# A four-layer graph network on one core: slot weights read from a PSUM bank, the last block's edges all on its list, the last-but-one update moved into the last turn

## The reference

```
s = x @ msg_w[:, :D].T ;  d = x @ msg_w[:, D:].T
messages = gelu(s[:, None, :] + d[None, :, :] + msg_b)
aggregated = einsum('ijd,ij->id', messages, adj)          # only where adj is not 0
new = concatenate([x, aggregated]) @ upd_w.T + upd_b
h = gelu(new) + x
out = layernorm(layernorm(h) * ln_w + ln_b + x)           # the layer's, then the network's
```

## Time and profile before

| | us |
|---|---|
| median of 3 runs | 740.55 (735.58 to 743.03) |
| the profiled execution's own time | 736.55 |
| its span, first to last instruction | 734.8 |
| layer 3's gathers, first to last | 445.91 to 709.27 |
| the last layer norm's end (DVE) | 728.0 |

### The profile page before, as it was taken

How to read it: one execution, slowest core, us unless ns; L and a number is a source line. 1 busy time by engine, 2 the same in 40 slices (tenths; PEclk the granted TensorE clock), 3 DMA queues, 4 the chain that set the end, 5 groups by cost and what they waited for, 6 DMA issues and landing times.

```text
span 734.8 us, 6845 instructions
## 1 busy us (share of the span) xinstructions
PE 455.6 (62%) x1987; PEld 268.9 (37%) x1987; DVE 503.4 (69%) x1592; ACT 302.4 (41%) x362; POOL 378.1 (51%) x499
## 2 busy tenths in 40 slices
PE   4122015999959999999998368665345542675211
PEld 3121012444425565544446356443133321433100
DVE  3409904998971754997054586899898879877744
ACT  3566256356942523399836031123223223322213
POOL 7303630667561030667000665777777777777740
PEclk9555555799989999999999759877567766655555
DMA  8999993799980020499601232212221222212200
GB/s 330 336 427 424 401 413 77 270 406 401 392 336 10 1 76 1 151 383 424 275 1 43 66 91 63 51 48 59 56 55 50 56 58 58 56 48 58 55 15 14
DMA packets 33211, 120.06 MB, mean 163 GB/s; under 512 B 8704, under 2 KB 19892, under 8 KB 24148
## 3 DMA queue, kind: packets, MB, share of 16 engines
q1 hardware_dynamic: 20258, 80.99, 28.0%
q0 software_dynamic: 10176, 38.57, 16.7%
q10 hardware_dynamic: 2734, 0.01, 0.2%
HBM read 114.00 MB, written 5.55 MB: 163 GB/s over the span
## 4 chain that ended last, share of the span: by engine, by line
PE 39%; POOL 20%; DMA 15%; DVE 10%; issue 8%; ACT 3%; SPq 3%; ACTq 0%; POOLq 0%
PE ps L121 37%; POOL G L919 16%; DMA ring<-in_adjT_dram 13%; POOL Go L919 4%; SPq L839 2%; DVE agg L1824 1%; DMA xT_s<-in_xT_dram 1%; PE ps L1254 1%; PE ps L1260 1%; ACT binT L998 1%; DVE G L1821 1%; PE ps L1375 1%; DVE I L1500 1%; DVE listed L1708 1%; DVE V L1510 0%
## 5 line engine op out<-in xcount | busy, mean ns | idle before, releaser
L919 POOL DMA_INDIRECT G<-near,IX x154 | 159.5, 1036 | 46.9 <-issue 46.3
L121 PE MATMUL ps<-ring,hwu 128*128 128x512 f32 (+3 forms) x264 | 114.7, 588 | 1.0 <-ACT hwu L1011 1.0
L121 PE MATMUL ps<-ring,xT_s 128*128 128x512 f32 (+2 forms) x264 | 106.9, 547 | 1.8 <-DMA ring<-in_adjT_dram 1.8
L121 PE MATMUL ps<-ident,agg 128*128 128x128 f32 (+1 forms) x44 | 14.9, 435 | 123.4 <-DVE agg L1824 123.4
L1500 DVE FIND_INDEX8 I<-V,rows 128x8 uint32<-128x340 f32 (+2 forms) x176 | 88.2, 504 | 0.0
L1510 DVE MAX8 V<-rows 128x8 f32<-128x340 f32 (+2 forms) x176 | 85.6, 497 | 0.8
L121 PE MATMUL ps<-E,M 128*128 128x321 f32 (+2 forms) x192 | 66.1, 505 | 16.8 <-DVE IO L1716 9.9
L121 PEld LDWEIGHTS ps<-ring,hwu 128*128 128x128 f32 (+1 forms) x264 | 51.3, 204 | 64.4 <-issue 63.3
L998 ACT ACTIVATE binT<-ring 128x2708 bf16<-128x2708 f32 (+1 forms) x22 | 53.9, 2457 | 47.5 <-DMA ring<-in_adjT_dram 47.5
L942 POOL DMA_DIRECT2D rows<-in_adj_dram x18 | 10.8, 603 | 120.5 <-DVE I L1500 120.5
L121 PE MATMUL ps<-u,binT 128*128 128x4 bf16 (+1 forms) x484 | 18.2, 167 | 82.7 <-ACT binT L998 82.7
(11 more groups left out here) (255 smaller groups left out, 858.5 us busy)
## 6 DMA issues: line engine op xcount, KB each, us to landing
ring<-in_adjT_dram SPq DMA_DIRECT2D x48, 1354.0 KB, 16.8
rows<-in_adj_dram POOLq DMA_DIRECT2D x17, 1354.0 KB, 10.3
rows<-in_adj_dram SPq DMA_DIRECT2D x4, 1354.0 KB, 23.3
G<-near,IX POOLq DMA_INDIRECT x154, 2.5
xT_s<-in_xT_dram SPq DMA_DIRECT2D x1, 1354.0 KB, 6.0
near<-hwu SPq DMA_DIRECT2D x1, 1344.0 KB
out_dram<-yo SPq DMA_DIRECT2D x21, 64.0 KB, 1.7
near2f<-hwu SPq DMA_DIRECT2D x5, 256.0 KB
```

The costliest lines, as they stand in the source:

```text
L121: return pe.matmul(dst, lhsT, rhs, start=start, stop=stop, skip_group_check=True)
L919: pool.indirect_dma_start(out=dst, out_offset=None, in_=table, in_offset=bass.IndirectOffsetOnAxis(ap=index, axis=0), engine_sem=o_g).then ...
```

## The change

The slots' weights are copied once by ScalarE into PSUM bank 2, and DVE's product (L1821) reads them there instead of in `T8`. To free that bank, the own shares use banks 0 and 1 by turns instead of 0 to 2, and those of pair g + 1 are put in turn g. The last block (20 rows) puts all its edges on the list, so that POOL gathers nothing for its slots, and its product is one `tensor_scalar` over the diagonal slot alone; in the last pair it comes first. `update(9)` and its square roots stand in turn 10, between the two blocks. POOL waits for `v_opre` of one turn earlier than before.

```diff
+        slot_weights = bank(SLOT_BANK, 0, NB * 8).rearrange("p (n k) -> p n k", k=8)
...
+        def pair3(g):
+
+            return (2 * g, 2 * g + 1) if g < NG3 - 1 else (2 * g + 1, 2 * g)
+
+        def turn3(n):
+            return 2 * (n // 2) + pair3(n // 2).index(n)
+
+        def first_slot(n):
+            return 0 if n < NB - 1 else TOP
@@ gpsimd
-                if g:
-                    pool.wait_ge(v_opre, g)
+                if g >= 2:
+                    pool.wait_ge(v_opre, g - 1)
-                for n in (2 * g, 2 * g + 1):
+                for n in range(2 * g, min(2 * g + 2, NB - 1)):
@@ scalar
+            act.wait_ge(v_win, 1)
+            act.activation(slot_weights, T8[:, :, :], ACT.Copy).then_inc(c_slots, 1)
...
+                n, later = pair3(g)
                 messages_listed(g)
-                messages(2 * g)
-                if 0 < g < NG3 - 1:
+                messages(n)
+                if g:
                     deviations3(g - 1)
-                messages(2 * g + 1)
+                messages(later)
                 aggregated(g)
-                if g == NG3 - 1:
-                    deviations3(g - 1, 0, 1)
                 features(g)
-            deviations3(NG3 - 2, 1, 2)
@@ tensor
-                aggregate(2 * g)
-                aggregate(2 * g + 1)
-                if g + 2 < NG3:
-                    own_shares(g + 2)
+                for n in pair3(g):
+                    aggregate(n)
+                if 0 < g < NG3 - 1:
+                    own_shares(g + 1)
                 new_features(g)
@@ vector
-                dve.match_replace(edges[0:r, n, SEGS * 8:2 * SEGS * 8], T8[0:r, n, :], V, 0.0)
+                if n < NB - 1:
+                    dve.match_replace(edges[0:r, n, SEGS * 8:2 * SEGS * 8], T8[0:r, n, :], V, 0.0)
+                else:
+                    dve.tensor_copy(edges[0:r, n, SEGS * 8:2 * SEGS * 8], V)
...
+                if first_slot(n) == TOP:
+                    dve.wait_ge(p_agg, turn3(n) - 1)
+                    dve.tensor_scalar(agg[0:r, n % 2, :], at[:, TOP, :], T8[0:r, n, TOP:TOP + 1], None, ALU.mult).then_inc(v_agg, 1)
+                    return
+                if n == 0:
+                    dve.wait_ge(c_slots, 1)
-                few.done(dve.tensor_tensor(at, at, T8[0:r, n, :].unsqueeze(2).broadcast_to([r, TOP + 1, D]), ALU.mult))
+                few.done(dve.tensor_tensor(at, at, slot_weights[0:r, n, :].unsqueeze(2).broadcast_to([r, TOP + 1, D]), ALU.mult))
...
-                aggregate(2 * g)
-                if 0 < g < NG3 - 1:
+                aggregate(n)
+                if g:
                     update(g - 1)
-                before_gelu(2 * g + 1)
+                before_gelu(later)
...
-            update(NG3 - 2)
             dve.wait_ge(v_out, NG3 - 1)
             update(NG3 - 1)
```

More of the change, by code:

```diff
@@ L44 @@
 LEAD3 = 3
+SLOT_BANK = 2
 PAIRS = 11
@@ L292, in build @@
         c_neg, c_dinv, c_d = sem("c_neg"), sem("c_dinv"), sem("c_d")
+        c_slots = sem("c_slots")
         c_msg, c_msgo, c_aggS, c_h = sem("c_msg"), sem("c_msgo"), sem("c_aggS"), sem("c_h")
@@ L1138, in _ @@
                                ACT.Copy).then_inc(c_d, 1)
+            act.wait_ge(v_win, 1)
+            act.activation(slot_weights, T8[:, :, :], ACT.Copy).then_inc(c_slots, 1)
             def messages(n):
-                act.wait_ge(v_pre, n + 1)
-                at = G3[0:rn(n), n % QUEUE3, :, :]
+                act.wait_ge(v_pre, turn3(n) + 1)
+                at = G3[0:rn(n), n % QUEUE3, first_slot(n):, :]
                 act.activation(at, at, ACT.Gelu).then_inc(c_msg, 1)
@@ L1158, in features @@
                     act.wait_ge(v_h, g)
-                act.activation(hh[:, :, :], bank(g % 3).rearrange("p (b w) -> p b w", w=2 * D)[:, :, D:2 * D], ACT.Gelu).then_inc(c_h, 1)
+                act.activation(hh[:, :, :], bank(g % 2).rearrange("p (b w) -> p b w", w=2 * D)[:, :, D:2 * D], ACT.Gelu).then_inc(c_h, 1)
             def deviations3(g, first=0, last=2):
@@ L1392, in own_shares @@
             def own_shares(g):
-                if g >= 3:
-                    pe.wait_ge(c_h, g - 2)
+                if g >= 2:
+                    pe.wait_ge(c_h, g - 1)
                 if g < NG3 - 1:
-                    last = mm(pe, bank(g % 3), ident[:, :], E2[:, 2 * g:2 * g + 2, EDGE:EW], True, True)
+                    last = mm(pe, bank(g % 2), ident[:, :], E2[:, 2 * g:2 * g + 2, EDGE:EW], True, True)
                 else:
@@ L1400, in own_shares @@
                         n = 2 * g + i
-                        last = mm(pe, bank(g % 3, i * 2 * D, 2 * D)[0:rn(n), :], ident[0:rn(n), 0:rn(n)], E2[0:rn(n), n, EDGE:EW], i == 0, True)
+                        last = mm(pe, bank(g % 2, i * 2 * D, 2 * D)[0:rn(n), :], ident[0:rn(n), 0:rn(n)], E2[0:rn(n), n, EDGE:EW], i == 0, True)
                 last.then_inc(p_pr, 1)
@@ L1422, in aggregate @@
                 r = rn(n)
-                pe.wait_ge(v_agg, n + 1)
-                mm(pe, bank(SUMS, n % 2 * P, r), agg[0:r, n % 2, :], ident[0:r, 0:r], False, n % 2 == 1).then_inc(p_agg, 1)
+                pe.wait_ge(v_agg, turn3(n) + 1)
+                mm(pe, bank(SUMS, n % 2 * P, r), agg[0:r, n % 2, :], ident[0:r, 0:r], False, turn3(n) % 2 == 1).then_inc(p_agg, 1)
             def new_features(g):
@@ L1429, in new_features @@
                     n = 2 * g + i
-                    at = bank(g % 3, (2 * i + 1) * D, D)[0:rn(n), :]
+                    at = bank(g % 2, (2 * i + 1) * D, D)[0:rn(n), :]
                     last = mm(pe, at, aggS[:, g % 2, i * P:i * P + rn(n)], u2T_s[:, :], False, True)
@@ L1810, in before_gelu @@
                 r, q = rn(n), n % QUEUE3
-                own = bank(n // 2 % 3, n % 2 * 2 * D, D)[0:r, :]
+                own = bank(n // 2 % 2, n % 2 * 2 * D, D)[0:r, :]
                 dve.wait_ge(p_pr, 2 * CH + n // 2 + 1)
-                dve.tensor_tensor(G3[0:r, q, TOP, :], pd3[0:r, n, 0:D], own, ALU.add)
+                alone = dve.tensor_tensor(G3[0:r, q, TOP, :], pd3[0:r, n, 0:D], own, ALU.add)
+                if first_slot(n) == TOP:
+                    alone.then_inc(v_pre, 1)
+                    return
                 dve.wait_ge(s_g[q], past2[q] + 16 * TOP * (n // QUEUE3 + 1))
@@ L1819, in aggregate @@
                 r, at = rn(n), G3[0:rn(n), n % QUEUE3, :, :]
-                dve.wait_ge(c_msg, n + 1)
-                few.done(dve.tensor_tensor(at, at, T8[0:r, n, :].unsqueeze(2).broadcast_to([r, TOP + 1, D]), ALU.mult))
+                dve.wait_ge(c_msg, turn3(n) + 1)
+                if first_slot(n) == TOP:
+                    dve.wait_ge(p_agg, turn3(n) - 1)
+                    dve.tensor_scalar(agg[0:r, n % 2, :], at[:, TOP, :], T8[0:r, n, TOP:TOP + 1], None, ALU.mult).then_inc(v_agg, 1)
+                    return
+                if n == 0:
+                    dve.wait_ge(c_slots, 1)
+                few.done(dve.tensor_tensor(at, at, slot_weights[0:r, n, :].unsqueeze(2).broadcast_to([r, TOP + 1, D]), ALU.mult))
                 if n >= 2:
-                    dve.wait_ge(p_agg, n - 1)
+                    dve.wait_ge(p_agg, turn3(n) - 1)
                 dve.tensor_reduce(agg[0:r, n % 2, :], at.rearrange("p k d -> p d k"), AX.X, ALU.add).then_inc(v_agg, 1)
@@ L1833, in _ @@
             for g in range(NG3):
+                n, later = pair3(g)
                 listed_before_gelu(g)
-                before_gelu(2 * g)
+                before_gelu(n)
                 if g + 3 < NG3:
                     rows_to_list(g + 3)
-                aggregate(2 * g)
-                if 0 < g < NG3 - 1:
+                aggregate(n)
+                if g:
                     update(g - 1)
-                before_gelu(2 * g + 1)
+                before_gelu(later)
                 if g + 1 < NG3:
                     list_to_rows(g + 1)
-                aggregate(2 * g + 1)
+                aggregate(later)
                 if g + 2 < NG3:
```

## The result

Median 716.92 us (716.03 to 719.41, four runs) against 738.07 us for the kernel before (735.01 to 743.03, four runs): ratio 0.9722 [0.9679, 0.9765]. The profiled execution took 716.03, its span 714.3 us; before it was 734.8, so 20.5 us of span went away. Forecast were 722 and, for the profiled execution, 718.3.

A forecast was written before the change was run, and what follows sets the result against it. POOL's gathers were taken to set layer 3's pace, with the end after them. Gains of 8.7 and 9.6 us, 18.3 off the profiled 736.55, gave 718.3; with the median 4.0 above, 722, range 715 to 732.

The forecast's parts named there:

- Part 1: Product's slot weights in PSUM, layer 3: 10.05 us of gather stalls removed, less new stalls; 8.7 us gain forecast.
- T: Start of L1815, the seven-slot add, for pair 9's first block; 677.17 before, 668.5 forecast.
- The mechanism: On POOL, a DVE operation with two SBUF inputs, already running at a gather's start, holds it; 17 gathers, 10.05 us.
- the new stalls elsewhere: Shifted gathers meeting DVE's other two-SBUF-input operations; bounded so that the gain lies between 5 and 10.05 us.
- The first rival's rule: `tensor_tensor` doesn't stall descriptor writing, so long gathers stay and only Part 2 acts: 731 us, chance 0.10.
- Part 2: Reordered end of layer 3, from T to the last norm: 50.8 to 41.2 us, 9.6 us gain, between 8 and 11.6.
- `hh`: ACT's Gelu after a pair's new features: first at T + 20.7, the last pair's at T + 35.9.
- the small product: Last block's one-slot product on DVE in the last turn: 0.3 us, done at T + 22.0.
- signs of being wrong: Trace signs against the forecast: L1821 at 1.5 or more, gathers held past L1815-like operations, DVE waiting for ACT in turn 10.
- the update's move: `update(9)` between the last turn's blocks: 5.2 us, to T + 27.2, previously behind everything with its table loads.
- Rivals 2 to 4: Slower PSUM weights, 731 to 733, chance 0.06; rival 3; stalls back elsewhere, 727, counted within the forecast's 0.82.
- rival 3: Own shares, now behind the aggregates on PE, hold L1813 every turn; slower than before, 748 us, chance 0.02.

The follow-up runs named there:

- x7: Changed kernel with the product's weights back in SBUF and own shares ahead of the aggregates on PE; 728.0 us beside 739.2 for the kernel before, ratio 0.9872.
- x8: Changed kernel with four small POOL memsets ahead of each block's seven gathers; 718.5 us beside 739.2 for the kernel before, ratio 0.9766.
- e2: Changed kernel with the product's weights read from SBUF again, so Part 2 alone; 771.7 us beside 790.7 for the kernel before, ratio 0.976.
- e3: Changed kernel with operands swapped: the seven-slot add reads own shares from SBUF, the product PSUM weights; 795.0 us beside 790.7 for the kernel before.
- e5: Changed kernel with `update(9)` put back behind the last turn, the list kept; 795.7 us beside 795.4 for the kernel before, ratio 1.000.
- e6: Changed kernel with the last block gathered and in the old order, the moved update kept; 801.5 us beside 795.4 for the kernel before.
- e4: Changed kernel with the next pair's own shares ahead of the two aggregates on PE; 795.1 us, repeated at 798.0; ratios 1.004 and 0.999.
- Part 1 alone: Kernel before with PSUM weights and own shares in two banks, old ending; 797.6 us, repeated at 803.5; ratios 1.007 and 1.005.
- r1: Kernel before, unchanged, run again for a trace in the slow surroundings; 783.5 us, one run.

## Why the prediction was right, and where its steps were off

**Part 1.** 8.7 us forecast, 9.2 measured: T went from 677.17 to 667.04, 10.13 us, of which 0.91 is that the first gather starts earlier (445.0 for 445.91). The sum had no term for that, and it looks like scatter: x7's first gather starts at 445.93 and x8's at 444.26. The mechanism is the one named: the 17 holds of 10.05 us went whole, and L1848 costs what L1821 did. The term that was mis-sized is the new stalls elsewhere, 1.35 us forecast: the other lines' holds up to the 174th gather rose from 4.34 (14.39 - 10.05) to 5.04, 0.7 us. That it came out so small is in part luck, since x8 has 7.05. The prediction also calls all those lines operations with two SBUF inputs; L1699 and L1722, 18 of the held gathers before, are `tensor_scalar` with one SBUF tile and values per row, so its rule was too narrow. And POOL did wait once in the earlier trace rows, 0.6 us for L1807: its idle time was 47.9 us, 47.3 of it issue. The period came to 22.9 us, from 598.23 to 621.10 and to 644.01 between the waits at L1836.

**The first rival's rule.** The Trainium skill, "SBUF — State Buffer", section "Who interferes with whom", gives as inferred that a `tensor_tensor` doesn't stall the writing of descriptors. Taken as a rule for these gathers, as the first rival does, it fails: 16 of 16 gathers are held in e2, 19 of 19 in x7 and, with the operands swapped, 8 of 8 in e3. The other half of what the Trainium skill says there, that two SBUF inputs contend with a GpSimd instruction that reads SBUF, fits the runs: a gather reads its indices there (`IX`, `IO`). Whether it is held at that read or at its descriptors no run here can tell.

**Part 2.** 9.6 us forecast, 10.3 measured (T + 50.8 to T + 40.5). Every step came in its place and none was off by over 0.8: L1831 at T + 18.9 (own shares at 19.1 forecast), `hh` at T + 20.4 (20.7), the small product's end T + 21.5 (22.0), `update(9)` to T + 26.6 (27.2), the last sum T + 32.1 (32.8), the second `hh` T + 35.1 (35.9), the last norm T + 40.5 (41.2). The new features and the two Gelus overlap at their edges by a few tenths, which I had added end to end. From the last norm to the end of the span are 6.8 us, as forecast. One of the prediction's signs of being wrong, that DVE in turn 10 waits for ACT, came true, with 2.00 us before L1844 and 3.10 before the last L1767. It was badly chosen: the prediction's own steps have DVE behind both of these Gelus.

**What the sum hid.** I counted the update's move as a gain, "before, these 5.2 us and their table loads lay behind everything", and e5 and e6 show that it isn't one where the gathers are not late. With the tails of the slow surroundings, the 10.2 us divide so: 9.4 are waits for the gathers of the last two blocks (34.58 to 25.2); the own shares behind the aggregates cost 1.2 (25.2 to 26.41); the last block's shorter work gives 3.4 (26.41 to 23.04); and the move costs 1.3 (23.04 to 24.36). Where POOL sets the pace the seven gathers of block 20 would be late by part of that without the move: POOL ends the last of them at 687.85 and a pair's turn starts 1.6 us after that, as at T in the rows before, at 689.4, while without the move L1836 would want them at 688.7 (the small product's end, 688.50, and L1831). By this estimate the move costs 0.6 us there, not 1.3; that kernel wasn't timed there. The forecast was right on the sum since the steps were laid out one behind another as the new order has them, whatever they were credited to.

**The median.** For the profiled execution 718.3 was forecast and 716.03 measured: 0.5 us from part 1, 0.7 from part 2 and 0.9 from the earlier first gather. For the median 722 was forecast and 716.92 measured, and most of that is another term: the prediction took the median to lie 4.0 above the profiled execution, as before, and it lay 0.9 above. Nothing in the record gives that a cause beside the scatter of the runs.

**Rivals 2 to 4.** PSUM weights are not slower (1.21 us). Own shares behind the aggregates are late only in the last turn, by 2.05 us on L1831 and 1.2 to 1.3 on the end; the other turns have no wait at L1831, so rival 3 had the right place and no size. The stalls came back only for 0.7 us.

**What stays open.** What pauses DVE, PE and ACT in the slow surroundings; why part 2 alone gains some 2% there and the kernels with weights in PSUM don't; and whether own shares first, on top of the change, gain their 1.3 us where POOL sets the pace, since no run of e4 met such surroundings. Part 1 alone was never timed there either. Where POOL sets the pace no kernel here was measured to beat the changed one; in the slow surroundings e2 was 3% faster than e3 and e4, all three one edit away from the changed kernel.

## What to carry to other kernels

When GpSimd's gathers pace a kernel, lay their starts beside DVE's timeline: if the long ones all end the same time after a DVE operation with two SBUF inputs, put one input of the longest such operation in PSUM (here that cost DVE nothing, 1.21 us for 1.22). A gain on the pacing engine is worth its full size only while it paces, and where it doesn't the same edit can even cost (e2 against e3 and e4); look in the profile of the surroundings that matter whether it still does. To learn what each half of a change to the end is worth, measure one chain with each half alone, since a step that is moved under one cover may have left another.

## What was not expected of the hardware

- A hold lasts until 0.81 to 0.83 us after the end of the DVE operation, nearly the 0.94 us that a gather takes. So it looks as if a held gather stops some 0.13 us after its start (0.94 - 0.81, an estimate). A product with both inputs in SBUF that starts inside a gather is not slowed: it took 1.21 to 1.23 us. The exception is a gather that starts 0.02 us after the product: in five such cases (three in r1, one each in e2 and x7) the gather took its 0.94, and the product 1.27 to 1.28.
- Not only `tensor_tensor` holds: in the changed kernel L1717, a `tensor_scalar` of 128x512 with one SBUF tile as input (0.47 to 0.60 us long), does too: the gather at 455.09 took 1.19 us, while the reduce L1851, 1.87 us long with one SBUF tile, held none of the 20 gathers that started in it in x7.
- The same program takes 717 or 799 us by its surroundings, with pauses of up to 20 us in three engines at once, and the kernel before 738 or 779 to 816 us.
